# Feed-forward layers with their hidden features on the partitions, and a state-space unit whose scores follow its third chunk

## The chip, the cores and the metric

The kernel runs on one core of one Trainium2 chip. The metric is the time of one execution on the device, in microseconds (us). Before the change its median over three runs is 1958.67 us (1956.84 to 1959.5).

## What is computed

Two sequences (b = 0, 1) of 1024 tokens with 256 features pass through two layers. A layer normalises its input, computes a sequence mixer and a feed-forward network on the normalised input, and adds mixer × silu(network) to the residual. Layer 0 has linear attention (4 key heads, 16 query heads of 128) and a mixture of 8 experts (176 hidden features each, the two best per token) plus a shared expert of 352 hidden features. Layer 1 has a state-space model of 32 heads of 64 (a decayed running state) and a quantised feed-forward network with 704 hidden features.

```python
# layer 0's network
combine = zeros.at[token, topk_idx].add(topk_w)
act = silu(gu[..., :F]) * gu[..., F:]                       # F = 176, eight experts
y = einsum('tef,te,ehf->th', act, combine, down_weights)
y = y + (silu(sgu[:, :Fs]) * sgu[:, Fs:]) @ shared_down.T   # Fs = 352
# layer 1's network, with W = (wq - 128) * scale
_qlinear(silu(_qlinear(x, wq_gate, s_gate)) * _qlinear(x, wq_up, s_up), wq_down, s_down)
# layer 1's mixer, per head and step
states = states * dec + xt[..., None] * bt[:, :, None, :]
yt = einsum('bhpn,bhn->bhp', states, ct) + xt * D
```

## The kernel before

Each sequence goes through seven phases, and all engines meet at the end of each (`end_phase`): normalisation; layer 0's network; attention; its output projection, which also normalises for layer 1; layer 1's network; the state-space (SSM) phase; its output projection. The order of work on each engine is written out by hand and held together by semaphores. A full-precision product of the normalised input is made of three passes over halves of the operands (`three_passes`: hi·hi, hi·lo, lo·hi), so every weight has a hi part (made by ScalarE, ACT) and a lo part (made by GpSimd, POOL, with `split_lo`, or by VectorE, DVE).

**The two networks.** The hidden features are worked on in groups of 352 (`FG`): five groups in layer 0 (four pairs of experts and the shared expert), two in layer 1. For each group the loop runs over eight chunks of 128 tokens, with tokens on the partitions (`ffn_group`, L540 in TensorE's block). Per chunk TensorE (PE) does `gate_up` (2 × 6 matmuls with 352 columns, L491), `hid_turn` (three transposes of the hidden values, L519) and `down` (nine matmuls with 256 columns, L532). ACT does the silu (L854) and copies the transposed values (L860). DVE multiplies by the up part and by the expert's weight of the token, a scalar on each partition (L1208, L1212), makes the lo part (L1219), and adds the chunk's result to `gate` in SBUF (L1241). The gate/up weights of a group (704 KB) share the buffer `w_raw` with all other projections. In layer 1 DVE first dequantises them with the scales (L1250, L1465). The silu of the sum is taken in the next phase (L887).

**The SSM phase.** It runs over 16 pairs of heads, and each pair over two units u of four chunks. PE's order within a unit is `ssm_unit` (L794): per chunk j a projection `project_xz`, `ssm_update` (L778) and `ssm_outputs` (L787, L792); behind chunk 0 the next unit's `project_b`, behind chunk 1 its `project_c`; in chunk 2, between the projection and the update, its scores `unit_scores` (L768, 16 small matmuls); in chunk 3 the transposes `b_turn` (L751). The scores need ACT's copy `c_copy` (L1114), and ACT takes its steps in order too: in the first unit of a pair it also makes the hi part of the next pair's weights (`ssm_prep`, L838), for which `w_raw` must have landed. SP issues that load behind `pdec` (L372), and `pdec` waits for the state of the previous pair's last chunk (L1522, a memset on DVE). DVE's order in a unit is per chunk `ssm_next_state` (L1527), `add_skip` (L1539), then in chunks 0 and 1 a scan (L1499), in chunk 2 `c_decayed` (L1507) and `decayed_scores` of head 0 (L1515), in chunk 3 that of head 1. `ssm_outputs` of a chunk waits until `add_skip` has read the chunk before it out of the one PSUM bank, and `add_skip` waits for POOL's `xd` (L463), which stands in POOL's queue behind the lo part of the next weights (L473).

## Time and profile before

| | |
|---|---|
| median of three runs | 1958.67 us |
| the profiled execution, and its span | 1956.97 us, 1955.2 us |
| PE, weight loads, DVE, ACT, POOL busy | 91%, 81%, 60%, 43%, 31% of the span |
| granted TensorE clock, mean | 0.97 |
| chain that ended last | PE 63%, DVE 9%, issue 8%, DMA 7%, ACT 6%, POOL 4%, SP's queue 2% |
| DMA | 110.83 MB, 57 GB/s on average |

The busy share of PE alone says little, since the ends of matmuls are modelled and overlap; what counts is how far apart the starts of its instructions are and where it stands idle. The page cuts the span into 40 slices, and the same pattern of slices comes twice, once for each sequence.

### The profile page before, as it was taken

To read this page: it belongs to the slowest core of one execution; us is meant where nothing else is said; L and a number is where in the kernel's file an instruction comes from. 1 tells how busy PE (TensorE), PEld (TensorE's weight loads), DVE (VectorE), ACT (ScalarE), POOL (GpSimd) and SP (SyncE) were. 2 spreads that over 40 slices of the span, in tenths; PEclk is the share of its full clock that TensorE was granted. 3 is DMA by queue.
4 is the path that set the end of the run, shared out by engine and by line. 5 is a ranking of instruction groups with operands and counts; after the bars stand their busy time and mean duration, and the time that the engine had idled before them with its cause. 6 is when DMAs were issued, how large, how long until landed. Compare 5 with 4: busy or idle time off the path is not lost.

```text
span 1955.2 us, 33861 instructions
## 1 busy us (share of the span) xinstructions
PE 1783.1 (91%) x11888; PEld 1591.4 (81%) x11888; DVE 1178.2 (60%) x2476; ACT 843.7 (43%) x2294; POOL 611.6 (31%) x768
## 2 busy tenths in 40 slices
PE   5998999899899999998969979998988999999989
PEld 4997777788888888887849967777888888888878
DVE  5555888554456566666455558885554556666664
ACT  4234445323344444445533344453233444444465
POOL 1012444001255555551010124440002555555510
PEclk9999999999999999998969999999999999999989
DMA  2120000002322222220021200000023222222200
GB/s 81 47 105 17 17 17 24 11 1 74 89 90 90 90 90 90 90 92 10 12 80 40 105 17 18 17 24 11 1 74 90 90 90 90 90 91 94 90 6 17
DMA packets 49783, 110.83 MB, mean 57 GB/s; under 512 B 5712, under 2 KB 14544, under 8 KB 49104
## 3 DMA queue, kind: packets, MB, share of 16 engines
q1 hardware_dynamic: 49616, 108.66, 16.8%
q8 instruction: 98, 1.61, 0.3%
q14 instruction: 69, 0.57, 0.1%
HBM read 106.02 MB, written 2.62 MB: 56 GB/s over the span
## 4 chain that ended last, share of the span: by engine, by line
PE 63%; DVE 9%; issue 8%; DMA 7%; ACT 6%; POOL 4%; SPq 2%; DVEq 0%; POOLq 0%; ACTq 0%
PE ps L491 23%; PE ps L563 11%; DMA w_raw<-in_w_in 6%; PE ps L532 5%; PE ps L768 4%; PE ps L787 4%; PE ps L555 3%; PE ps L778 2%; POOL rb L417 2%; PE ps L663 2%; PE ps L644 2%; PE ps L519 2%; PE ps L664 2%; PE ps L792 2%; SPq L372 2%
## 5 line engine op out<-in xcount | busy, mean ns | idle before, releaser
L468 POOL TENSOR_TENSOR y<-yg,sz 128x128 f32<-128x128 f32 x256 | 209.8, 820 | 262.2 <-DVE yg L1539 262.2
L563 PE MATMUL ps<-w_out,yT 128*128 128x256 f32 x1024 | 226.1, 379 | 0.0
L1527 DVE SCALAR_TENSOR_TENSOR ssm_state<-ssm_state,pdec,ps 64x64 f32<-64x64 f32 x448 | 125.2, 279 | 165.7 <-PE ps L778 159.1
L563 PEld LDWEIGHTS ps<-w_out,yT 128*128 128x128 f32 x1024 | 192.5, 190 | 24.9
L417 POOL TENSOR_TENSOR rb<-ra,rb 128x512 f32<-128x512 f32 x80 | 118.6, 1482 | 221.9 <-DVE rb L1367 221.8
L787 PE MATMUL ps<-xz_x,mt 128*128 128x128 f32 x1024 | 167.5, 282 | 2.6 <-DVE mt L1515 1.4
L1499 DVE TENSOR_TENSOR_SCAN lmat<-dec,ident 128x512 f32<-128x512 f32 x128 | 155.9, 1218 | 0.4 <-issue 0.4
L491 PE MATMUL ps<-w_in_hi,xnT_hi 128*128 128x256 f32 x512 | 155.5, 304 | 0.0
L1539 DVE TENSOR_TENSOR yg<-ps,xd 128x128 f32<-128x128 f32 x256 | 74.6, 291 | 128.7 <-issue 88.8
L854 ACT ACTIVATE silu_g<-ps 128x352 f32<-128x352 f32 x112 | 51.7, 465 | 228.6 <-PE ps L491 228.5
L491 PE MATMUL ps<-gu_hi,xnT_hi 128*128 128x352 f32 x448 | 148.9, 332 | 0.0
L491 PE MATMUL ps<-gu_lo,xnT_hi 128*128 128x352 f32 x448 | 148.5, 331 | 0.0
L787 PEld LDWEIGHTS ps<-xz_x,mt 128*128 128x128 f32 x1024 | 140.5, 192 | 8.6 <-DVE mt L1515 6.7
L491 PE MATMUL ps<-gu_hi,xnT_lo 128*128 128x352 f32 x448 | 147.2, 329 | 0.0
L491 PE MATMUL ps<-w_in_lo,xnT_hi 128*128 128x256 f32 x512 | 144.2, 282 | 0.0
L491 PE MATMUL ps<-w_in_hi,xnT_lo 128*128 128x256 f32 x512 | 143.6, 280 | 0.0
L463 POOL TENSOR_TENSOR xd<-xz_x,d_row 128x128 f32<-128x128 f32 x256 | 122.5, 479 | 34.7 <-ACT xz_x L1126 34.7
L1131 ACT ACTIVATE xw<-ps,lmat 128x64 f32<-128x64 f32 x512 | 133.1, 319 | 0.0
L1126 ACT ACTIVATE xz_x<-ps 128x128 f32<-128x128 f32 x256 | 71.6, 280 | 141.1 <-PE ps L491 129.6
L1208 DVE SCALAR_TENSOR_TENSOR hid<-ps,combine_g,silu_g 128x176 f32<-128x176 f32 x160 | 56.3, 394 | 113.0 <-ACT silu_g L854 98.6
L473 POOL TENSOR_TENSOR w_in_lo<-w_raw,w_in_hi 128x256 fp32r<-128x256 f32 x120 | 87.3, 727 | 92.7 <-ACT w_in_hi L838 92.7
L1000 ACT ACTIVATE ra<-rb 128x512 f32<-128x512 f32 x80 | 50.4, 630 | 148.6 <-POOL rb L417 147.5
(170 smaller groups left out, 4809.1 us busy)
## 6 DMA issues: line engine op xcount, KB each, us to landing
dec<-dec_dram SPq DMA_DIRECT2D x64, 512.0 KB, 5.1
w_raw<-in_w_in SPq DMA_DIRECT2D x32, 512.0 KB, 4.3
pdec<-dec_dram SPq DMA_DIRECT2D x128, 128.0 KB, 2.9
w_raw<-in_gu SPq DMA_DIRECT2D x14, 704.0 KB, 4.2
w_raw<-in_w_qkv SPq DMA_DIRECT2D x8, 768.0 KB, 4.9
dn_raw<-in_dn SPq DMA_DIRECT2D x14, 384.0 KB, 4.8
w_out<-in_w_o SPq DMA_DIRECT2D x2, 2048.0 KB, 11.9
w_out<-in_w_out SPq DMA_DIRECT2D x2, 2048.0 KB, 8.5
```

What stands on the lines that cost most here:

```text
L417: nc.gpsimd.tensor_tensor(rb[:, k], ra[:, k], rb[:, k], ALU.add).then_inc(a_rot.sem, 1)
L463: nc.gpsimd.tensor_tensor(xd[:, s].rearrange("p (h c) -> p h c", c=64), xz_x[:, s, :].rearrange("p (h c) -> p h c", c=64)[:, 0:4:3, :], d_ ...
L468: nc.gpsimd.tensor_tensor(y[:, c, bass.ds((2 * i + w) * P, P)], yg[:, s], sz[:, s], ALU.mult).then_inc(s_out.sem, 1)
L473: ins = nc.gpsimd.tensor_tensor(w_in[1 - w][1][:, k, half], raw[:, k, half], w_in[1 - w][0][:, k, half], ALU.subtract)
L491: mm = nc.tensor.matmul(out, left(l, k), right(r, k), start=(j == 0), stop=(j == len(steps) - 1))
L532: mm = nc.tensor.matmul(ps[:, 6 + c % 2, 0:DM], hidT[l][:, c % 2, t * P:(t + 1) * P], dn[slot][r][:, t, :], start=(j == 0), stop=(j == len ...
L563: mm = nc.tensor.matmul(ps[:, 4 + s, 0:DM], yT[:, s, t, :], w_out[:, t, :], start=(t == 0), stop=(t == NT - 1))
L768: mm = nc.tensor.matmul(ps[:, 4 + h, j * P:(j + 1) * P], bT[q, toks], cT[q, toks], start=True, stop=True)
L787: nc.tensor.matmul(out, mt1[:, u % 2, h, c % 4 * P:(c % 4 + 1) * P], xz_x[:, c % 2, h * P:(h + 1) * P], start=(h == 0), stop=False)
L1131: ins = nc.scalar.activation(xw[:, s, 64 * h:64 * h + 64], ps[:, 2 + s, 64 * h:64 * h + 64], ACT.Copy, scale=lmat[:, h, (c + 1) * P - 1:(c ...
L1499: nc.vector.tensor_tensor_scan(lmat[:, h, toks], dec[:, h, toks], ident4[:, 0:HALF], 0.0, ALU.mult, ALU.add).then_inc(s_scan.sem, 1)
L1527: ins = nc.vector.scalar_tensor_tensor(ssm_state[q, nxt, q], ssm_state[q, cur, q], pdec[q, (c + 1) * P - 1:(c + 1) * P], ps[q, 7, q], ALU. ...
```

## The change

- **Networks.** The hidden features are now on the partitions: tiles of 128 features (14 in layer 0, of which three are the shared expert with 32 rows of padding in the third, and eleven hold the 8 × 176 expert features without a gap; 6 in layer 1, the last with 64 features whose gate and up rows share one product). Per tile and half of the tokens (a unit u) PE does 12 matmuls with 512 columns and 12 with 256; the result of all tiles is summed up in four PSUM banks. No transposes and no adding in SBUF are left.
- A token's weight for an expert is no longer a scalar on a partition. The table is transposed by PE once per sequence (8 matmuls), written to DRAM, and each expert tile loads its rows of it, broadcast over the partitions (`comb`, 512 KB per tile). POOL multiplies the silu by it.
- The weights of a tile (384 KB) have buffers of their own (`fw_raw`, two deep). ACT and POOL (layer 1: ACT and DVE) split them in two pieces, 512 and 256 columns wide, one in each unit. In layer 1 the zero point goes off while splitting, the scales are applied by the silu, by the split of the hidden values and in the last sum.
- In layer 0 the silu of the sum is taken at the end of the phase out of PSUM; in layer 1 DVE applies the last scale out of PSUM at the end of the phase.
- **SSM phase.** On PE `unit_scores` moves behind the update and the outputs of chunk 2. On DVE `decayed_scores` of head 0 moves from the end of chunk 2 to the start of chunk 3.
- Two constants (`s_gu`, `s_dn`) are loaded at the start. Logits of the router and of the decays use PSUM banks 2 and 3.

```diff
@@ TensorE: networks
-                for j in range(2):
-                    mm = three_passes(ps[:, 2 * (c % 2) + j, 0:FG],
-                                      lambda l, k: xnT[l][:, k, c * P:(c + 1) * P],
-                                      lambda r, k: weights[r][:, k, j * FG:(j + 1) * FG])
+                pe.wait_ge(f_hid.sem, f_hid.done(u - 2))
+                for j in range(1 if together else 2):
+                    mm = three_passes(ps[:, 2 * hf + j, :],
+                                      lambda l, kk: fw[k % 2][l][:, (2 * kk + j) * P:(2 * kk + j + 1) * P],
+                                      lambda r, kk: xnT[r][:, kk, hf * HALF:(hf + 1) * HALF])
...
+            def down(b, k, hf, first, last, rows=P):
+                pe.wait_ge(f_hi.sem, f_hi.done(u))
+                pe.wait_ge(f_lo.sem, f_lo.done(u))
+                for j in range(4):
+                    c = 4 * hf + j
+                    for x, (l, r) in enumerate(SPLITS):
+                        mm = nc.tensor.matmul(ps[:, 4 + c // 2, (c % 2) * DM:(c % 2 + 1) * DM], hidT[l][0:rows, hf, j * P:(j + 1) * P],
+                                              fw[k % 2][r][0:rows, KT * 2 * P:FW], start=(first and x == 0 and c % 2 == 0),
+                                              stop=(last and x == 2), skip_group_check=True)
...
+                gate_up(b, 0, 1)
+                for u in range(2 * NF0):
+                    if u == 2:
+                        pe.wait_ge(own_dve, 2 * b + 2)
+                        pe.wait_ge(f_hid.sem, f_hid.done(2 * b * NF + 2))
+                        for c in range(NC):
+                            mm = nc.tensor.matmul(ps[0:NE, c // 4, c % 4 * P:(c % 4 + 1) * P], combine[:, c, :], ident4[:, 0:P],
+                                                  start=True, stop=True)
+                        mm.then_inc(rt_combT.sem, 1)
+                        down(b, 1, 0, False, False)
+                        pe.wait_ge(rt_combcopy.sem, rt_combcopy.done(b))
+                        gate_up(b, 2, 0)
+                        continue
+                    if u + 2 < 2 * NF0:
+                        gate_up(b, (u + 2) // 2, u % 2)
+                    down(b, u // 2, u % 2, u < 2, u >= 2 * NF0 - 2)
@@ TensorE: SSM unit
-                        if ahead and j == 2:
-                            unit_scores(u + 1, nhf)
                         ssm_update(u, m, c)
                         ssm_outputs(u, m, c)
...
+                        if ahead and j == 2:
+                            unit_scores(u + 1, nhf)
@@ VectorE: SSM unit
+                        if ahead and j == 3:
+                            decayed_scores(u + 1, 0)
                         ssm_next_state(m, c)
                         add_skip(m, c)
...
                         if j == 2:
                             c_decayed(u + 1)
-                            decayed_scores(u + 1, 0)
@@ ScalarE: layer 0's network
+                for u in range(2 * NF0):
+                    k, hf = u // 2, u % 2
+                    if u > 0:
+                        silu(b, k, hf)
+                    if u == 2:
+                        act.wait_ge(rt_combT.sem, rt_combT.done(b))
+                        nc.scalar.activation(comb_T[:].rearrange("p (h t) -> p h t", h=2), ps[0:NE, 0:2, :], ACT.Copy).then_inc(rt_combcopy.sem, 1)
+                    hidden_hi(b, k, hf)
+                    if hf == 0 and k + 1 < NF0:
+                        weights_hi0(b, k + 1, 0)
+                    if hf == 1 and k + 1 < NF0:
+                        weights_hi0(b, k + 1, 1)
@@ GpSimd: layer 0's network
+                for k in range(NF0):
+                    e = k - SHARED_TILES
...
+                    for hf in range(2):
+                        u = 2 * (b * NF + k) + hf
+                        if e >= 0:
+                            pool.wait_ge(f_silu.sem, f_silu.done(u))
+                            nc.gpsimd.tensor_tensor(silu_g[:, hf, :], silu_g[:, hf, :], comb[:, e % 2, hf * HALF:(hf + 1) * HALF], ALU.mult).then_inc(f_comb.sem, 1)
+                        if k + 1 < NF0:
+                            weights_lo(k + 1, hf)
@@ VectorE: networks
+                nc.vector.tensor_tensor(hid[0:rows, hf, :], up, silu_g[0:rows, hf, :], ALU.mult).then_inc(f_hid.sem, 1)
...
+                    ins = nc.vector.tensor_tensor(hidT[1][0:rows, hf, :], hid[0:rows, hf, :], hidT[0][0:rows, hf, :], ALU.subtract)
@@ SP: layer 0's network
+                for k in range(NF0):
+                    ffn_weights(b, k, a["fw0"][F0[k]])
...
+                    if k >= SHARED_TILES:
+                        e = k - SHARED_TILES
+                        sp.wait_ge(f_comb.sem, f_comb.done(2 * (b * EXPERT_TILES + e - 2) + 1))
+                        for x, (row, p0, p1) in enumerate(expert_rows(F0[k])):
+                            sp.dma_start(comb[p0:p1, e % 2, :], comb_dram[row:row + 1, :].broadcast_to([p1 - p0, T])).then_inc(comb_in[e % 2], 16)
@@ ScalarE: layer 1's network
+                for u in range(2 * NF1):
+                    silu(b, NF0 + k, hf, s_gu[0:rows, k, 0:1], rows)
+                    hidden_hi(b, NF0 + k, hf, s_gu[0:rows, k, 1:2], rows)
+                    if k + 1 < NF1:
+                        weights_hi1(b, k + 1, hf)
+                    if k == NF1 - 1 and hf == 0:
+                        first_pair()
```

## Rows read from the trace of the kernel before

**Rows 1.** Busy time by stage: PE, PEld, DVE, ACT, POOL, granted clock, DMA share.

```profile
22.30:171.30 149.00, 142.70 (x981) 136.28 (x981) 80.04 (x182) 47.85 (x95) 16.81 (x8) 0.99 0.15 55
...
440.20:512.70 72.50, 63.89 (x396) 61.04 (x396) 34.59 (x61) 22.29 (x40) 7.70 (x5) 0.89 0.31 92
512.70:897.60 384.90, 359.85 (x2784) 326.87 (x2784) 232.07 (x532) 177.91 (x624) 202.65 (x316) 1.00 0.26 84
```

**Rows 2.** Timeline of PE, layer 0's network: start us, us, what, [idle before].

```profile
41.14 0.32 PE L491 MATMUL ps<-gu_hi,xnT_hi 128*128 128x352 f32 x1
...
43.07 0.49 PE L519 MATMUL ps<-ident,hid 128*128 128x128 f32 x3
...
44.47 0.32 PE L491 MATMUL ps<-gu_hi,xnT_hi 128*128 128x352 f32 x1
```

**Rows 3.** Timeline where PE or ACT stood idle in both networks and behind.

```profile
35.91 0.90 PE L519 MATMUL ps<-ident,hid 128*128 128x128 f32 x3 [4.51 <-DVE hid L1208]
...
181.87 1.28 ACT L887 ACT_TABLE_LOAD   x1
...
465.47 0.55 PE L519 MATMUL ps<-ident,hid 128*128 128x128 f32 x3 [2.77 <-DVE hid L1212]
...
496.09 1.06 ACT L838 ACTIVATE w_in_hi<-w_raw 128x1024 fp32r<-128x1024 f32 x1 [7.80 <-issue]
...
498.11 0.90 PE L519 MATMUL ps<-ident,hid 128*128 128x128 f32 x3 [4.03 <-DVE hid L1212]
```

**Rows 4.** Groups of instructions: xcount | busy us, mean ns | idle before.

```profile
L473 POOL TENSOR_TENSOR w_in_lo<-w_raw,w_in_hi 128x256 fp32r<-128x256 f32 x120 | 87.3, 727 | 92.7 <-ACT w_in_hi L838 92.7
L1515 DVE TENSOR_TENSOR mt<-ps,lmat 128x512 f32<-128x512 f32 x128 | 86.8, 680 | 0.7 <-PE ps L768 0.7
...
L768 PE MATMUL ps<-cT,bT 64*128 64x128 f32 x1024 | 74.5, 285 | 43.8 <-ACT cT L1114 43.8
...
L389 POOL TENSOR_TENSOR w_qkv_lo<-w_raw,w_qkv_hi 128x512 fp32r<-128x512 f32 x24 | 30.4, 1285 | 58.3 <-ACT w_qkv_hi L838 58.3
...
L838 ACT ACTIVATE w_qkv_hi<-w_raw 128x512 fp32r<-128x512 f32 x24 | 14.0, 625 | 0.0
```

**Rows 5.** Timeline of PE in one pair of SSM heads.

```profile
632.26 1.16 PE L768 MATMUL ps<-cT,bT 64*128 64x128 f32 x16
633.35 0.49 PE L778 MATMUL ps<-xw,b_tok 128*128 128x128 f32 x2
...
644.22 1.16 PE L768 MATMUL ps<-cT,bT 64*128 64x128 f32 x16 [1.08 <-ACT cT L1114]
...
645.63 0.61 PE L787 MATMUL ps<-xz_x,mt 128*128 128x128 f32 x4
...
646.30 0.60 PE L751 MATMUL ps<-ident,bT 128*128 128x128 f32 x4
```

**Rows 6.** Timeline of SP, DVE, ACT and POOL in the same pair.

```profile
637.37 0.58 SPq L303 DMA_DIRECT2D w_raw<-in_w_in  x1
...
633.98 0.57 DVE L1527 SCALAR_TENSOR_TENSOR ssm_state<-ssm_state,pdec,ps 64x64 f32<-64x64 f32 x2 [2.31 <-PE ps L778]
...
636.04 0.17 DVE L1522 MEMSET ssm_state<- 128x128 f32 x1
...
643.76 0.29 DVE L1539 TENSOR_TENSOR yg<-ps,xd 128x128 f32<-128x128 f32 x1 [2.69 <-issue]
...
641.39 1.06 ACT L838 ACTIVATE w_in_hi<-w_raw 128x1024 fp32r<-128x1024 f32 x1 [3.44 <-DMA w_raw<-in_w_in]
...
643.22 0.45 POOL L463 TENSOR_TENSOR xd<-xz_x,d_row 128x128 f32<-128x128 f32 x1
```

**Rows 7.** Timeline of POOL and of DVE, one stretch in which both work.

```profile
72.95 3.25 POOL L389 TENSOR_TENSOR gu_lo<-w_raw,gu_hi 128x1408 fp32r<-128x1408 f32 x1 [24.18 <-ACT gu_hi L838]
...
73.63 3.38 DVE L1223 TENSOR_TENSOR dn_lo<-dn_raw,dn_hi 128x768 fp32r<-128x768 f32 x1 [0.87 <-ACT dn_hi L879]
```

**Rows 8.** Part 6 of the page, DMA issues: count, KB each, us to landing.

```profile
dec<-dec_dram SPq DMA_DIRECT2D x64, 512.0 KB, 5.1
```

More of the change, by code:

```diff
@@ L39 @@
 FE = 176
-FG = 2 * FE
-G0, G1 = NE // 2 + 1, 2
-GRP = G0 + G1
-DT = 3
+SHARED = 2 * FE
+NF0 = 14
+EXPERT_TILES = NE * FE // P
+F0 = tuple(range(EXPERT_TILES, NF0)) + tuple(range(EXPERT_TILES))
+SHARED_TILES = NF0 - EXPERT_TILES
+HID = 704
+NF1 = 6
+NF = NF0 + NF1
+FW = KT * 2 * P + DM
 HP = 16
@@ L54, with expert_rows @@
 PHASES = 7
-CONSTS = 7
-RAWS = G0 + KVH + G1 + HP
+CONSTS = 9
+RAWS = KVH + HP
 PARTS = 3
-def split_ffn0(b, g):
-    return b * (RAWS + (PARTS - 1) * KVH) + g
 def split_qkv(b, i, part):
-    return split_ffn0(b, G0) + PARTS * i + part
-def split_ffn1(b, k):
-    return split_qkv(b, KVH, 0) + k
+    return b * (PARTS * KVH + HP) + PARTS * i + part
 def split_ssm(b, h):
-    return split_ffn1(b, G1) + h
+    return b * (PARTS * KVH + HP) + PARTS * KVH + h
+def expert_rows(tile):
+    f, rows = tile * P, []
+    while f < tile * P + P:
+        end = min((f // FE + 1) * FE, tile * P + P)
+        rows.append((f // FE, f - tile * P, end - tile * P))
+        f = end
+    return rows
+COMB_LOADS = [sum(len(expert_rows(t)) for t in range(k, EXPERT_TILES, 2)) for k in range(2)]
 class Event:
@@ L536, in ffn_group, with gate_up @@
-            def ffn_group(b, g, slot, weights, split, last=False):
-                for c in range(NC):
-                    if c + 2 < NC or not last:
-                        g2, c2 = following(g, c, 2)
-                        gate_up(b, g2, c2, weights[c + 2 >= NC], split + (c + 2 >= NC))
-                    if c + 1 < NC or not last:
-                        hid_turn(b, *following(g, c, 1))
-                    down(b, g, c, slot)
+            def gate_up(b, k, hf, together=False):
+                n = b * NF + k
+                u = 2 * n + hf
+                if hf == 0:
+                    pe.wait_ge(f_wgh.sem, f_wgh.done(n))
+                    pe.wait_ge(f_wgl.sem, f_wgl.done(n))
+                pe.wait_ge(f_hid.sem, f_hid.done(u - 2))
[3 more added lines that the diff above has]
+                                      lambda r, kk: xnT[r][:, kk, hf * HALF:(hf + 1) * HALF])
+                mm.then_inc(f_gu.sem, 1)
@@ L1607, in launch_arrays, with tile_rows @@
     g["router"] = np.concatenate([rows_to_k(f["L0_ffn_gate_weight"]).reshape(P, -1), np.zeros((P, DM - KT * NE), np.float32)], 1)
-    def groups(gate_up, down):
-        gus = np.stack([rows_to_k(x).reshape(P, -1) for x in gate_up])
-        dns = np.stack([rows_to_k(np.concatenate([x, np.zeros((DM, DT * P - FG), x.dtype)], 1)).reshape(P, -1) for x in down])
-        return gus, dns
+    def tile_rows(gate, up, down):
+        return np.concatenate([rows_to_k(np.concatenate([gate, up])).reshape(P, -1), np.concatenate([down.T, np.full((P - down.shape[1], DM), PAD, down.dtype)])], 1)
@@ L1623, in launch_arrays @@
+    g["s_gu"] = scales.transpose(1, 0, 2)
     g["s_dn"] = f["L1_ffn_s_down"].reshape(1, DM)
```

445 lines of the change are left out of this document (184 added, 261 removed).

## The prediction

> **What bounds the kernel now.** I read three views in this order. First the stages [rows 1]. In the SSM phase PE is busy for 360 of 385 us at full clock. In layer 1's network it is busy for 64 of 72.5, at a granted clock of 0.89. So PE is the bound, with idle stretches, and what is worth something is work taken from PE, or idle time of it.
>
> Second the timeline of PE. In layer 0's network a chunk of 128 tokens takes 44.47 - 41.14 = 3.33 us from start to start [rows 2]. Its 12 gate/up matmuls take 43.07 - 41.14 = 1.93 us, that is 0.161 each or 0.457 ns a column; by the column a matmul of 512 columns takes 0.234 and one of 256 takes 0.117 (estimates from that row). Nine down matmuls are then 1.05, so the three transposes and their change of operand cost 0.35 us of PE in each chunk. The idle stretches are 4.5 us behind the router, while DVE ranks the experts, and 2.8 and 4.0 us in layer 1's network [rows 3]. In the second of these ACT sat in its queue at the SSM phase's first weights for 7.8 us, and silus stood behind them.
>
> Third the SSM phase. PE waits 43.8 us before the scores for ACT's cT [rows 4], once per pair of heads (384.9 / 16 = 24.06 us a pair). The pair at 632 us shows the loop that sets this [rows 5, 6]: DVE clears the state of the last chunk (636.04), only then SP may issue pdec and behind it the weights (637.37), these land before 641.39 (ACT waited 3.44), ACT splits them, then come its copies of the chunk and of b and c, and PE starts its scores at 644.22 after 1.08 us of idling. POOL's xd at 643.22 and DVE's yg at 643.76 hang on the same landing. Over the two sequences 14 pairs each do so, a mean of 43.8 / 28 = 1.56 us.
>
> **Layer 0's network, work of PE.** Before: 40 chunks of 3.33 = 133.2 us. After: 14 tiles of 24 × 0.234 + 24 × 0.117 = 8.42, together 117.9. That is -15.3 per sequence. The loads of weights into PE fall from 24 per chunk to 48 per tile and hide as before.
>
> **Its start.** The 4.5 us idle stretch goes. What is late next: ACT now loads the table of silu, of exp and of silu again (1.28 us each, as the row at 181.87 in [rows 3]), and DVE's first product stands ahead of the ranking, so that the second gate/up product waits some 1.2 us for DVE to have read the logits; the third waits for the weights that ACT splits only behind exp: 1.5 us. Then comes the turned table of expert weights: 8 small products of two passes each (16 × 0.11 = 1.8 us by the 0.35 / 3 of a transpose), and in this unit ACT copies the table (about 1.0) before it may make the hi part of the hidden values, so that PE's next down product waits: copy 1.0, hi 0.63, lo 0.68 and handovers = 2.5. Sum -4.5 + 1.2 + 1.5 + 1.8 + 2.5 = +2.5 (between 0 and +6). The four small waits between groups (not shown; between 0 and 2 in all) count as -1.5.
>
> **The expert tiles: a ring through four engines.** Here I expect the new bound. POOL's product with `comb` must be between silu and DVE's product, ACT takes silu, hi part and the weights' hi part in that order, and POOL's lo part of the weights stands ahead of its next product. With durations from [rows 4] (ACT 512 columns 0.63, POOL 512 columns 1.28, 256 columns 0.73, DVE 0.68, hand-over about 0.07, ACT overlapping its next start by 0.1), counted from the end of POOL's product: DVE's product until 0.82, ACT's hi until 1.52, DVE's lo part until 2.27; ACT's weights until 2.05 (512 wide) or 1.8. Can POOL work beside DVE's lo part, which reads two SBUF operands? No [rows 7]: DVE's step at 73.63 took 3.38 us instead of some 1 us, ending 0.8 behind POOL's at 72.95 + 3.25; so the later of the two waits for the earlier one's end. So POOL begins at 2.2: 2.2 + 1.28 + 1.28 = 4.76 in the first unit, 2.2 + 0.73 + 1.28 = 4.21 in the second, 8.97 a tile against PE's 8.42. Eleven tiles × 0.55 = +6.0 per sequence. Lower bound 0 (POOL beside DVE: 4.6 + 3.8 = 8.4, PE is the bound again); upper bound with POOL's products held once more for a DVE step of 0.68 in each unit +1.4 a tile, +21. I take 6.0, since DVE has no second step of that kind in the unit.
>
> The Trainium skill (SBUF — State Buffer, section "Who interferes with whom") says that a VectorE instruction with two SBUF inputs and a GpSimd one that reads SBUF exclude each other for a whole instruction, while one with a single SBUF input doesn't. The trace agrees with the first half; by the second half DVE's product out of PSUM costs the ring nothing more. Without that rule the ring would be 8.4 and the forecast 12 us lower.
>
> **Its end.** The sum's silu out of PSUM stands behind the last product (two of 0.53, where one short addition stood): +1.1, an estimate. In return the attention phase loses a silu of 1.9 us and a table load there and back (the row at 181.87 in [rows 3]); it lay partly beside other work: -1.3 (0 to -4.5).
>
> **The broadcast loads** of `comb` are hidden: 512 KB took 5.1 us to land for `dec` [rows 8], they are issued when tile k-2 frees the buffer, three units (13 us) ahead of use, and the weights of the next tile (384 KB) go with them. Without that cover each tile would cost the landing, 5 us or more.
>
> **Layer 0's network in sum:** -15.3 + 2.5 - 1.5 + 6.0 + 1.1 - 1.3 = -8.5 per sequence.
>
> **Layer 1's network.** PE: before 16 × 3.33 = 53.3; after 132 × 0.234 + 144 × 0.117 = 47.7: -5.6. Both idle stretches go, -6.8: the weights come in pieces, and the SSM weights are awaited only beside the last tile, 8 units after their chain has begun. Part of the clock lost with them comes back: 0.11 of 72.5 us is missing, 5 us of it at half clock behind the start; I count -2.0. Against it: the second tile's weights are split behind the first tile's hidden values, 1.5; the last sum takes four DVE steps of 0.68 where a short addition stood, two of them behind PE's end: +1.5. POOL is out of this ring, whose ACT part is about 2.4 us against a unit of 4.21. Sum -11.4 (-7 to -14).
>
> **SSM phase.** After the change PE does the update and outputs of chunk 2 while it would have waited. The update can go at once (ACT copies its inputs ahead of b and c). The outputs need yg of chunk 1, read at 643.76 + 0.29 = 644.05: nearly the time at which cT came. So of the stall only the update is hidden: outputs from 644.12, 0.67 (645.63 to 646.30), scores 1.09 (644.22 to 645.31 is their share before), b_turn at 645.9 instead of 646.30: 0.40 earlier. The second gain is in the other unit of the pair, which has no stall. There the memset of the state came 3.78 us behind the start of the scores (632.26 to 636.04), because update, state step, yg and the masks followed them. Now update and outputs go first: state step at 0.63 behind the slot's start (633.35 to 633.98 before), yg at 1.2, c at 1.45, mask at 2.2 (as soon as the scores end at 2.15), memset at 2.87: 0.91 earlier, and with it SP's pdec and the weights. The loop shrinks by 1.31 us per pair; the stall had 1.56 on average, so it doesn't run dry. 14 × 1.31 = -18.3 per sequence. DVE's order is the same as before (head 0's mask stands right before chunk 3's state step in both). Nobody waits longer for the masks: the next unit's outputs come 0.7 and more behind them.
>
> **Normalisation and start:** two more constants ahead of x (each at most the 0.58 that SP took at 637.37 in [rows 6]), shorter splits beside the normalisation: 0 (-3 to +1).
>
> **Sum:** (-8.5 - 11.4 - 18.3) × 2 = -76.4. The profiled execution took 1956.97 (span 1955.2), so 1880.6; the median of three was 1.7 higher. I give 1881.
>
> **Rivals.** (a) PE is the bound everywhere: POOL isn't held by DVE (-6.0 per sequence) and the remaining SSM stall of 0.25 to 0.7 goes too (-5). For it: POOL's wait needs an exact overlap, and DMA landings vary. 1881 - 22 = 1859. (b) The scores' move gives only scraps: the loop is closed by something that doesn't move, such as POOL's queue, and 0.4 per pair is left: 28 × 0.9 = +25, 1906. For it speaks yg at 643.76, tied to the landing; against it that the landing itself follows the memset. (c) The expert ring is longer, 10 us a tile, by slow POOL steps: +23, 1904. (d) Slower than before: the gate on TensorE's clock. In layer 1's network, with 2.8 and 4.0 us of idling, the clock is 0.89; in the SSM phase with 1.1 us it is 1.00 [rows 1, 3, 5]. If the ring's idle parts (0.55 a tile) drop the clock, a tile takes 16.8 us: 11 × 2 × 7.9 = +173, 2054. It makes the kernel slower from 10 of the 22 tiles on. Against it: the stall per tile is smaller than those at clock 1.00.
>
> The Trainium skill (TensorE: Matmul & The Clock Gate, section "A second HAM failure mode: psum-queue depth-cycling") speaks for (d): short idling between groups of matmuls let the clock swing. The SSM rows here, with such gaps at 1.00, don't show it.
>
> **Chances.** Forecast 0.55 (1868 to 1893), (a) 0.20, (b) 0.13, (c) 0.08, (d) 0.04. The range 1843 to 1908 holds the forecast, most of (a), (b) and (c). What this kernel's measurement can tell from no change is about 0.2%. Faster 0.95, same 0.01, slower 0.04.
>
> **What would show it.** Layer 0's network (149.0) at about 140, expert tiles 9.0 apart, POOL's comb products starting as its weight step ends; layer 1's at 61 without idling at its SSM weights; the pair of heads at 22.7 with 0.2 to 0.7 of stall ahead of the outputs or scores; the memset 2.9 behind the update. Wrong if a tile takes 8.4 or over 9.5, if the stall before the scores stays above 1 us, or if landings of `comb` are waited for.

## The result, and the profile after

| | before | after |
|---|---|---|
| median | 1957.76 us (four runs) | 1885.9 us (1884.98 to 1886.98) |
| profiled execution, its span | 1956.97, 1955.2 | 1884.98, 1883.2 |
| ratio of times, 95% interval | | 0.9636 (0.9619 to 0.9653) |
| PE, DVE, ACT, POOL busy | 91%, 60%, 43%, 31% | 93%, 58%, 45%, 36% |

The forecast was 1881 (1843 to 1908). By phases, each cut where the last of ACT, DVE and POOL drains, first and second sequence:

| us | before | after | difference | forecast |
|---|---|---|---|---|
| normalisation | 22.3, 19.1 | 22.6, 15.8 | +0.3, -3.3 | 0 |
| layer 0's network | 148.9, 150.8 | 141.3, 140.7 | -7.6, -10.1 | -7.2 |
| attention | 190.9, 192.5 | 192.1, 191.4 | +1.2, -1.1 | -1.3 |
| layer 1's network | 72.6, 72.3 | 60.8, 61.1 | -11.8, -11.2 | -11.4 |
| SSM | 384.8, 384.1 | 370.5, 371.2 | -14.3, -12.9 | -18.3 |
| the two output projections | 157.2, 157.1 | 156.0, 156.9 | -1.2, -0.2 | 0 |

The stages of the changed kernel, first sequence (us of the stretch, busy time with counts, granted clock, DMA share, GB/s), against [rows 1]:

```profile
22.62:163.94 141.32, 130.83 (x708) 109.64 (x708) 45.44 (x68) 54.51 (x95) 61.00 (x52) 0.97 0.32 105
433.73:494.57 60.84, 55.08 (x288) 46.64 (x288) 30.52 (x45) 26.43 (x39) 3.38 (x2) 0.93 0.37 113
494.57:865.10 370.53, 361.23 (x2784) 326.96 (x2784) 230.78 (x532) 177.82 (x624) 203.04 (x316) 0.99 0.27 87
```

PE is busy for 361 of 370.5 us in the SSM phase where it was busy for 360 of 385: no work went, idle time did. In layer 1's network 55 of 60.8 us are left of 64 of 72.5.

**The expert tiles don't close at 8.97 us.** PE's down products of one half start at 86.82, 95.33 and 103.83: 8.50 us a tile. Timeline of POOL, DVE and ACT in one tile (start, duration, what, [idle before]):

```profile
95.37 0.94 POOL L396 TENSOR_TENSOR fw_lo<-fw_raw,fw_hi 128x256 fp32r<-128x256 f32 x1 [1.77 <-ACT fw_hi L873]
96.27 1.30 POOL L411 TENSOR_TENSOR silu_g<-silu_g,comb 128x512 f32<-128x512 f32 x1
99.56 1.29 POOL L396 TENSOR_TENSOR fw_lo<-fw_raw,fw_hi 128x512 fp32r<-128x512 f32 x1 [1.99 <-ACT fw_hi L870]
100.80 1.29 POOL L411 TENSOR_TENSOR silu_g<-silu_g,comb 128x512 f32<-128x512 f32 x1
...
95.02 0.69 DVE L1203 TENSOR_TENSOR hidT_lo<-hid,hidT_hi 128x512 fp32r<-128x512 f32 x1 [0.70 <-ACT hidT_hi L862]
97.60 0.69 DVE L1196 TENSOR_TENSOR hid<-ps,silu_g 128x512 f32<-128x512 f32 x1 [1.89 <-POOL silu_g L411]
99.00 0.69 DVE L1203 TENSOR_TENSOR hidT_lo<-hid,hidT_hi 128x512 fp32r<-128x512 f32 x1 [0.70 <-ACT hidT_hi L862]
...
98.33 0.63 ACT L862 ACTIVATE hidT_hi<-hid 128x512 fp32r<-128x512 f32 x1 [2.20 <-DVE hid L1196]
99.77 0.60 ACT L856 ACTIVATE silu_g<-ps 128x512 f32<-128x512 f32 x1 [0.29 <-PE ps L497]
```

From the end of POOL's product (96.27 + 1.30 = 97.57) DVE's product starts after 0.03, ACT's hi part after 0.76, DVE's lo part ends after 2.12 (99.00 + 0.69), POOL's 512-wide step starts at 1.99 and its next product ends at 4.52 (102.09). The other half takes 3.97, the sum is 8.50. The silu isn't on this chain: ACT waits 0.29 us for PE in front of it, and it still ends (100.37) 0.43 before POOL's product starts. But PE's own work is as long as the chain. A tile of the shared expert, which has no product on POOL, takes 8.48 us (PE's down products start at 61.33 and at 69.81). PE and the ring are level.

**The end of layer 0's network** has a stall that I had not foreseen. ACT waits 3.58 us for the first attention head's weights, two silus stand behind it, and PE then idles 3.53 us. SP had issued that load behind the tables and w_o, 3 MB in all, and it took 11.9 us to land. The clock falls in the idle time (0.89 on average between 152.0 and 155.7), and the last two groups of down products take 2.5 us each instead of 1.41. Timeline of ACT, then of PE:

```profile
149.88 1.67 ACT L840 ACTIVATE w_qkv_hi<-w_raw 128x512 fp32r<-128x512 f32 x3 [3.58 <-DMA w_raw<-in_w_qkv]
...
155.70 0.55 PE L533 MATMUL ps<-fw_hi,hidT_hi 128*128 128x256 f32 x1 [3.53 <-DVE hidT_lo L1203]
```

The stretch of the first group behind it (us of the stretch, busy times, granted clock, DMA):

```profile
155.70:158.20 2.50, 2.50 (x12) 2.50 (x12) 0.79 (x2) 0.63 (x1) 2.50 (x4) 0.50 0.00 0
```

**Start of the SSM phase.** The first projections run at half clock. Their starts are 0.43 apart, at full clock 0.23. In the kernel before they ran at a clock of 1.00. Timeline of PE:

```profile
495.21 0.63 PE L497 MATMUL ps<-xnT_lo,w_in_hi 128*128 128x512 f32 x1
495.64 0.63 PE L497 MATMUL ps<-xnT_hi,w_in_lo 128*128 128x512 f32 x1
```

**A pair of heads.** The mean period is 23.0 us (24.1 before). The stall before the scores [rows 5] is gone, and a smaller one stands before the outputs of chunk 2: the update starts at 647.11 and the outputs only at 647.77, 0.66 later, where it is 0.22 at the other chunks, so 0.44 is lost; the distances of starts in excess of the usual make 7.2 us at this place in the first sequence and 8.1 in the second. What it waits for can be followed backwards: yg at 647.34, POOL's xd at 646.78, behind POOL's lo part of the weights at 646.08, behind ACT's hi part, behind the landing of weights that SP issued only after the memset. Timeline of the engines in this order of steps, headed by the update of the unit before:

```profile
636.36 0.38 PE L780 MATMUL ps<-xw,b_tok 128*128 128x128 f32 x2
...
639.22 0.17 DVE L1477 MEMSET ssm_state<- 128x128 f32 x1
...
640.54 0.58 SPq L306 DMA_DIRECT2D w_raw<-in_w_in  x1
...
644.95 1.06 ACT L840 ACTIVATE w_in_hi<-w_raw 128x1024 fp32r<-128x1024 f32 x1 [2.87 <-DMA w_raw<-in_w_in]
...
646.08 0.74 POOL L479 TENSOR_TENSOR w_in_lo<-w_raw,w_in_hi 128x256 fp32r<-128x256 f32 x1 [2.21 <-ACT w_in_hi L840]
646.78 0.47 POOL L469 TENSOR_TENSOR xd<-xz_x,d_row 128x128 f32<-128x128 f32 x1
...
647.34 0.29 DVE L1494 TENSOR_TENSOR yg<-ps,xd 128x128 f32<-128x128 f32 x1 [2.13 <-issue]
...
647.11 0.38 PE L780 MATMUL ps<-xw,b_tok 128*128 128x128 f32 x2
647.77 0.68 PE L789 MATMUL ps<-xz_x,mt 128*128 128x128 f32 x4 [0.28 <-DVE yg L1494]
...
649.70 0.66 PE L753 MATMUL ps<-ident,bT 128*128 128x128 f32 x4
```

### The profile page after: what moved, and what is told of

Same layout as the page of the kernel before. It is cut to its first block, busy times and chain, and to the rows that moved or that the text cites. A ratio compares the mean times of both kernels' runs of the same rounds, so it can differ in the third digit from the quotient of the medians.

```text
span 1883.2 us, 31983 instructions
## 1 busy us (share of the span) xinstructions
PE 1742.3 (93%) x11128; PEld 1506.7 (80%) x11128; DVE 1091.5 (58%) x2215; ACT 854.1 (45%) x2288; POOL 679.6 (36%) x846
## 4 chain that ended last, share of the span: by engine, by line
PE 54%; issue 15%; DVE 14%; POOL 10%; ACT 5%; DMA 2%; SPq 1%; POOLq 0%; DVEq 0%; ACTq 0%
PE ps L497 20%; PE ps L554 12%; PE ps L789 4%; PE ps L546 3%; POOL silu_g L411 3%; PE ps L533 2%; PE ps L770 2%; POOL y L474 2%; PE ps L794 2%; POOL rb L429 2%; DVE yg L1494 2%; POOL fw_lo L396 2%; PE ps L664 2%; PE ps L665 2%; PE ps L645 2%
## 5 line engine op out<-in xcount | busy, mean ns | idle before, releaser
L1196 DVE TENSOR_TENSOR hid<-ps,silu_g 128x512 f32<-128x512 f32 (+1 forms) x80 | 55.2, 690 | 171.7 <-POOL silu_g L411 105.6
L396 POOL TENSOR_TENSOR fw_lo<-fw_raw,fw_hi 128x512 fp32r<-128x512 f32 (+1 forms) x56 | 62.7, 1120 | 249.3 <-ACT fw_hi L870 198.7
L497 PE MATMUL ps<-xnT_hi,fw_hi 128*128 128x512 f32 x312 | 125.8, 403 | 8.1 <-DVE fw_lo L1214 3.8
L497 PE MATMUL ps<-xnT_lo,fw_hi 128*128 128x512 f32 x312 | 124.6, 399 | 0.0
L497 PE MATMUL ps<-xnT_hi,fw_lo 128*128 128x512 f32 x312 | 124.0, 397 | 0.0
L497 PE MATMUL ps<-xnT_hi,w_in_hi 128*128 128x512 f32 x256 | 113.5, 443 | 4.5 <-DVEq L295 3.8
```

Source lines behind the costliest of these rows:

```text
L396: nc.gpsimd.tensor_tensor(fw[k % 2][1][:, cols], fw_raw[:, k % 2, cols], fw[k % 2][0][:, cols], ALU.subtract).then_inc(lo.sem, 1)
L497: mm = nc.tensor.matmul(out, left(l, k), right(r, k), start=(j == 0), stop=(j == len(steps) - 1))
```

## The experiments

The kernels were timed in three groups, each on one chip beside the kernel before, whose medians there were 1952.4, 1951.3 and 1949.2 us. The changed kernel, run again in the last group, has 0.9641 (0.9623 to 0.966), where it had 0.9636. A difference of ratios below is taken from 0.9638, times 1951 us. Each ratio's interval is some 3 us wide to either side, so a difference of two is uncertain by some 4. The lengths of phases and pairs come from one profiled execution of each kernel: the changed kernel's first one took 1885.0 us, that in the last group 1877.9.

### The scores' move, undone and alone

**Undone.** `unit_scores` stands again ahead of `ssm_update` and `ssm_outputs` of chunk 2, in both units of a pair:

```diff
+                        if ahead and j == 2:
+                            unit_scores(u + 1, nhf)
                         ssm_update(u, m, c)
                         ssm_outputs(u, m, c)
...
-                        if ahead and j == 2:
-                            unit_scores(u + 1, nhf)
```

> The changed kernel with the SSM scores back in their old place (ahead of the update and outputs of chunk 2); the networks stay as changed. By the forecast's own terms the move is worth 0.40 + 0.91 = 1.31 us a pair of heads, 36.6 us in all: 1885.9 + 36.6 = 1922.5 us. Rival 1: the move is worth less, 16.0 us a sequence (the phase became 13.6 shorter, and 2.4 us of that phase went to projections at half clock, which the networks' change brings and which stays here): 1918 us. Rival 2: the move is worth only the 13.6 us by which the phase shrank: 1913 us.

Measured: 0.9799 (0.9783 to 0.9815), that is +31.4 us. Rival 1 (32) fits; the 36.6 doesn't, and rival 2 (27) lies at the edge. Read the other way this is the kernel before with the networks' change alone: -39.2 us, where the forecast's two network terms make 39.8.

**Alone.** The same move made in the kernel before.

> The kernel before with the SSM move alone. Forecast: 1957.8 - 36.6 = 1921.2. Rival 1 (16.0 a sequence): 1925.8. Rival 2 (13.6 a sequence): 1930.6. Together with e1: if the parts are independent, the ratios of e1 and e4 multiply to that of the whole change, 0.9636. Here the SSM phase's first projections should run at full clock, as before.

Measured: 0.9837 (0.9822 to 0.9852), -31.8 us; rival 1 fits again, and the 36.6 lies outside the interval. The two ratios multiply to 0.9639: the parts add up. The SSM phase of the first sequence with the move alone (columns as in the first fence; before it is 384.9 at a clock of 1.00 [rows 1], after it 370.5 at 0.99, above):

```profile
515.20:881.00 365.80, 358.38 (x2784) 325.38 (x2784) 231.06 (x532) 178.03 (x624) 202.92 (x316) 1.00 0.27 89
```

The same phase in the changed kernel with the old order:

```profile
490.60:879.90 389.30, 363.67 (x2784) 330.00 (x2784) 231.66 (x532) 177.42 (x624) 202.44 (x316) 0.98 0.25 83
```

Both sequences together: 769.0 before and 733.9 with the move alone; 775.3 in the changed kernel with the old order and 741.8 with the new. So the move took 35.1 us from this phase in the one kernel and 33.5 in the other, where the forecast said 36.6. The networks' change made the phase longer, by 6.3 with the old order and by 7.9 with the new; some of this is the difference between executions, since the changed kernel in the last group has 736.9.

The mean clock of 1.00 in [rows 1] hides a part of this gain. From memset to memset a pair takes 23.87 us on average before and 22.78 with the move alone, 1.10 less, if the pairs in which the granted clock falls are left out. There are two of these before, 26.64 and 26.38 us long, and one with the move alone, of 25.63. In front of the two before, PE had waited 2.80 and 2.55 us for cT, the longest such waits there. For the first of them the timeline of PE, and the stretch behind it (columns as above):

```profile
669.39 1.16 PE L768 MATMUL ps<-cT,bT 64*128 64x128 f32 x16 [2.80 <-ACT cT L1114]
```

```profile
669.00:679.00 10.00, 9.59 (x67) 9.00 (x68) 6.81 (x15) 3.50 (x14) 6.58 (x10) 0.83 0.18 58
```

**One unit at a time.** The condition `and hf == 0` or `and hf == 1` on the moved call, the other unit's call back in front:

> The changed kernel with the scores moved only in the first unit of each pair of heads (chunks 0 to 3, the one in which PE waited for ACT's cT); in the second unit they are back in front. Forecast: this drops the 0.91 us a pair that came from the state being cleared earlier, 25.5 us: 1911.4. Rival: the gain sits in the first unit, where the update and the outputs fill the stall, and the second unit's order matters little: 1886 to 1890.

> The changed kernel with the scores moved only in the second unit of each pair (chunks 4 to 7, after which the state is cleared). Forecast: this drops the 0.40 us a pair, 11.2 us: 1897.1. Rival (the gain sits in the first unit): 1908 to 1913. If the two terms add up, what e2 and e3 lose sums to what e1 loses.

Measured: without the second unit's move 0.9776 (0.976 to 0.9791), +26.9 us, 0.96 per pair where the forecast had 0.91. Without the first unit's move 0.9629 (0.9615 to 0.9644), -1.8 us with an uncertainty of about 4: nothing, where the forecast had +11.2, and the rival, which had the gain in the first unit, is out. Together the two lose 25.1 us, where the old order in both units loses 31.4. The 6.3 between them is hardly more than the uncertainty, and long pairs are in it: with the old order three pairs have a fall of the clock, without the second unit's move one. The other pairs are 23.90 and 23.91 us long, so undoing the first unit's move as well costs nothing more. The first unit of a pair in the kernel without the first unit's move, ACT's split and PE's `b_turn`:

```profile
645.80 1.06 ACT L842 ACTIVATE w_in_hi<-w_raw 128x1024 fp32r<-128x1024 f32 x1 [3.25 <-DMA w_raw<-in_w_in]
...
650.71 0.60 PE L753 MATMUL ps<-ident,bT 128*128 128x128 f32 x4
```

From the start of ACT's split to `b_turn` it takes 650.71 - 645.80 = 4.91 us, in the changed kernel 649.70 - 644.95 = 4.75: the moved scores gain 0.16, not 0.40, as yg keeps the outputs waiting. At the memset nothing of it is left (17.04 us behind the split's start against 17.07).

### The ring, made longer

POOL makes each product with `comb` a second time, into a tile that nobody uses:

```diff
+                            nc.gpsimd.tensor_tensor(rt_gt[:].rearrange("p a e -> p (a e)"), silu_g[:, hf, :], comb[...], ALU.mult)
                             nc.gpsimd.tensor_tensor(silu_g[:, hf, :], silu_g[:, hf, :], comb[...], ALU.mult).then_inc(f_comb.sem, 1)
```

> The changed kernel with POOL's product with comb made twice in every unit of the expert tiles (the extra one goes to a scratch tile and is not used): 1.25 us more in the ring, per unit. In the changed kernel a tile takes 8.50 us, and POOL's products start right behind its split steps. If the ring has no slack left beside PE, a tile takes 8.50 + 2.5 = 11.0: 1885.9 + 55 = 1941. If PE alone sets 8.50 and the ring has the 0.25 us a unit that ACT waits for PE in front of each silu, 10.5: 1930. By the forecast's ring of 8.97, 11.5: 1952.

Measured: 0.9879 (0.9856 to 0.9902), +47 us; layer 0's network takes 165.7 and 165.9 us, +24.8 per sequence, 2.3 a tile on average. POOL's product that counts (L412; the extra one, L411, isn't shown) at the start of one tile and of the next:

```profile
107.00 1.28 POOL L412 TENSOR_TENSOR silu_g<-silu_g,comb 128x512 f32<-128x512 f32 x1
...
117.94 1.28 POOL L412 TENSOR_TENSOR silu_g<-silu_g,comb 128x512 f32<-128x512 f32 x1
```

The middle of the phase as one stretch:

```profile
70.00:170.00 100.00, 82.39 (x440) 70.05 (x439) 25.60 (x37) 27.92 (x55) 64.77 (x55) 0.97 0.35 115
```

The tile is 117.94 - 107.00 = 10.94 us long: the ring had hardly any slack (less than 0.1) and took nearly the whole 2.5. What it also shows: POOL's step of 256 columns takes 0.94 us here and in the changed kernel, where it overlaps DVE's lo part (95.37 against 95.02 + 0.69), and 0.73 for the same width alone [rows 4]. So DVE does hold POOL up, but by 0.2, less than the 0.34 that was left of DVE's step. By the rule of the Trainium skill cited in the prediction (SBUF — State Buffer, section "Who interferes with whom") it would have been all of it; the measurement decides.

The clock: PE is busy for only 82 of the 100 us here, and its granted clock is 0.97 on average. That mean hides falls. Between 65 and 170 us PE idles 2.24 to 2.26 us ahead of seven products of this ring; behind two of them (at 78.60 and 133.52) the clock goes to half for a while, behind the other five it doesn't. Timeline of PE for one of each, and the stretches behind them:

```profile
78.60 0.47 PE L498 MATMUL ps<-xnT_hi,fw_hi 128*128 128x512 f32 x1 [2.26 <-issue]
...
100.68 0.47 PE L498 MATMUL ps<-xnT_hi,fw_hi 128*128 128x512 f32 x1 [2.24 <-issue]
```

```profile
78.60:83.60 5.00, 5.00 (x17) 4.04 (x18) 1.38 (x2) 1.43 (x3) 3.23 (x3) 0.66 0.27 90
100.70:105.70 5.00, 5.00 (x28) 4.32 (x29) 1.38 (x2) 1.42 (x3) 3.23 (x3) 1.00 0.20 66
```

The tile with the fall takes 12.4 us and the next one 9.7, together only 0.2 more than twice 10.94: PE takes the lost time out of the idle time that it has here.

### Three orders

**The first head's weights earlier.** SP issues them ahead of tile 12's weights, not behind the tables and the 2 MB of w_o:

```diff
                 for k in range(NF0):
+                    if k == NF0 - 2:
+                        weights(split_qkv(b, 0, 0), a["w_qkv"][0], KT * QKV)
                     ffn_weights(b, k, a["fw0"][F0[k]])
...
-                for i in range(0, KVH):
+                for i in range(1, KVH):
```

> The changed kernel with one transfer moved: SP issues the first attention head's weights (768 KB) ahead of the weights of layer 0's tile 12, instead of behind the tables and the 2 MB of w_o. In the changed kernel they land at 149.88, ACT waits 3.58 us for them with two silus behind, and PE idles 3.69 us (3.63 in the second sequence) before the down products of tile 13. If that wait is the cause, both stalls go: 1885.9 - 7.3 = 1878.6. Rival: what is late next (POOL's products with comb behind its split steps, or w_raw competing with the loads of comb) keeps most of it: 1884 to 1886.

Measured: 0.9572 (0.9555 to 0.9589), -12.9 us; the phase takes 138.3 and 136.1 us, 7.6 less in both together. The 3.7 us stall is gone (stalls here are distances of starts in excess of the usual), and the one before the last down products grew from 1.6 to 2.7, since its silu and its product no longer had time to spare. The rest of the ratio's gain stands in phases that the edit doesn't touch, and its own five runs spread from 1863.4 to 1875.0, so I go by the phases. Both sequences idle alike before the last down products, but the clock falls only in the first. The first down product of each, and then the stretches behind it:

```profile
155.52 0.55 PE L535 MATMUL ps<-fw_hi,hidT_hi 128*128 128x256 f32 x1 [2.52 <-DVE hidT_lo L1205]
...
1088.50 0.35 PE L535 MATMUL ps<-fw_hi,hidT_hi 128*128 128x256 f32 x1 [2.54 <-DVE hidT_lo L1205]
```

```profile
155.50:158.00 2.50, 2.48 (x11) 2.50 (x12) 0.00 (x0) 0.00 (x0) 1.01 (x1) 0.50 0.36 44
1088.40:1091.00 2.60, 1.67 (x12) 1.49 (x12) 0.00 (x0) 0.80 (x2) 1.09 (x1) 1.00 0.25 45
```

**The next pair's weights earlier.** In the SSM phase SP issues them behind the first half's `pdec`:

```diff
-                    weights(split_ssm(b, h), a["w_in"][h], KT * XZBC)
+                    if h == 0:
+                        weights(split_ssm(b, h), a["w_in"][h], KT * XZBC)
...
                         for k in range(2):
                             sp.dma_start(pdec[64 * k:64 * k + 64, toks], ...).then_inc(pdec_in[hf], 16)
+                        if hf == 0 and h + 1 < HP:
+                            weights(split_ssm(b, h + 1), a["w_in"][h + 1], KT * XZBC)
```

> The changed kernel with SP's order in the SSM phase changed: the next head pair's weights are issued behind the first half's pdec, not behind the second half's, which waits for the state to be cleared. ACT waits 42.6 us per sequence for them now (3.0 a pair). Theory of the loop (memset, pdec, weights, split, scores, memset): it is cut, the waits before the outputs (7.2 us a sequence), before the scores (5.4) and the longer pairs of 23.6 to 24.1 go, the period falls from 23.0 to about 22.0: 1885.9 - 28 = 1858. Rival 1: PE's own work is the bound at 22.6 and only the odd pairs gain: 1875 to 1880. Rival 2: the transfers then collide with dec and pdec, which become what is awaited: 1886 or more.

Measured: 0.951 (0.9497 to 0.9522), -25 us; pairs are 22.00 us apart, nearly all of them. One stretch of the phase:

```profile
515.00:840.00 325.00, 324.62 (x2579) 298.37 (x2577) 217.88 (x491) 164.66 (x578) 187.71 (x294) 1.00 0.28 94
```

PE is busy for 324.6 of 325 us. The loop is shown: memset, pdec, weights and split set the pace, and with the weights issued ahead of the memset PE does.

**With the old order of the scores**, and the same early issue of the weights.

> The changed kernel with the SSM scores back in their old place, but with the next pair's weights issued behind the first half's pdec. Theory: the scores' move was worth 28 to 32 us only because it shortened the loop memset, pdec, weights, split, scores, memset; with that loop cut by the earlier issue, PE sets the pair at 22.0 us in either order: the ratio to the kernel before is that of the changed kernel with the early issue alone, 0.951, within 0.002. Rival: the move is also worth something by itself, as update and outputs fill the wait for ACT's cT: 0.957 or more (0.4 us a pair).

Measured: 0.9567 (0.9553 to 0.9581). My theory missed: with the loop cut the move is still worth 0.0057, 11 us. But the rival's mechanism isn't it either: PE has no wait for cT left. PE's own pitch differs, 22.27 against 22.00 us a pair. Timeline of PE in one unit with the new order:

```profile
570.01 0.28 PE L500 MATMUL ps<-w_in_hi,xnT_lo 128*128 128x256 f32 x1
570.13 0.38 PE L783 MATMUL ps<-xw,b_tok 128*128 128x128 f32 x2
...
571.11 1.16 PE L773 MATMUL ps<-cT,bT 64*128 64x128 f32 x16
572.21 0.66 PE L756 MATMUL ps<-ident,bT 128*128 128x128 f32 x4
572.62 0.36 PE L500 MATMUL ps<-w_in_hi,xnT_hi 128*128 128x256 f32 x1
```

The same in the old order:

```profile
571.39 0.28 PE L500 MATMUL ps<-w_in_hi,xnT_lo 128*128 128x256 f32 x1
571.65 1.16 PE L773 MATMUL ps<-cT,bT 64*128 64x128 f32 x16
572.74 0.49 PE L783 MATMUL ps<-xw,b_tok 128*128 128x128 f32 x2
...
573.74 0.60 PE L756 MATMUL ps<-ident,bT 128*128 128x128 f32 x4
574.10 0.36 PE L500 MATMUL ps<-w_in_hi,xnT_hi 128*128 128x256 f32 x1
```

The same instructions lie between the last projection pass in front and the first one behind: 572.62 - 570.01 = 2.61 us against 574.10 - 571.39 = 2.71, and all units between 515 and 840 us that have both ends in this stretch are alike to 0.01. In each unit the scores are the only products of 64 rows (64*128), the others have 128. Time goes where the shape changes. Going into the scores takes 0.14 more than a pass in the old order (571.39 to 571.65, where a pass is followed after 0.12), and the update behind them 0.11 more than in the new (0.33 to the outputs' start against 0.22); with `b_turn` behind them instead it is 0.05 (0.41 against 0.36), and in front 0.09 (0.31 behind the last outputs against 0.22). The Trainium skill (TensorEngine Tiling (Array Packing), section "Key Properties") says that a change of the tiling mode drains TensorE. The trace agrees in so far as the distances of starts are longer at these places. But both orders have two such changes in a unit, and no run here separates the change of shape from other causes, nor why one order pays 0.1 more. By the pitch of the pairs it is 0.27 × 28 = 8 us; the 11 come from ratios of two groups, uncertain by some 4.

**The hi part before the table's copy.**

```diff
                     if u == 2:
+                        hidden_hi(b, k, hf)
                         act.wait_ge(rt_combT.sem, rt_combT.done(b))
                         nc.scalar.activation(comb_T[:]..., ACT.Copy).then_inc(rt_combcopy.sem, 1)
-                    hidden_hi(b, k, hf)
+                    else:
+                        hidden_hi(b, k, hf)
```

> The changed kernel with ACT's hi part of the hidden values of unit 2 ahead of its copy of the turned table (1.01 us). If the 2.60 us that PE idles there come from that order, the idle time falls to 1.6; the next gate/up product then waits for the copy, which is hidden behind the down product of 1.4. Rival: it stays at 2.6, since the hi part waits for DVE's product, which comes late anyway.

Timeline of PE at that place, L396 being POOL's lo part of the weights:

```profile
48.85 0.47 PE L497 MATMUL ps<-xnT_hi,fw_hi 128*128 128x512 f32 x1 [1.54 <-POOL fw_lo L396]
```

The 2.6 us stall in front of the down product is gone, not just 1.0 of it, and 1.7 stand in front of the next gate/up product, which waits not for the copy but for POOL's lo part: tile 2's weights stood behind the copy on ACT. The phase takes 139.4 and 138.9 us, 1.8 less in each sequence. There is one execution of this kernel, and its time of 1871.6 us is not used.

**All three, with tile 2's weights also ahead of the copy.**

> The changed kernel with three orders changed: the first attention head's weights issued ahead of tile 12, the next head pair's weights in the SSM phase issued behind the first half's pdec, and ACT's copy of the turned table put behind its hi parts of unit 2 and of tile 2's weights. From the runs with the first two alone -7 and -25 us, and for the third the whole stall of 2.6 in each sequence, -5: 1885.9 - 37 = 1849, ratio 0.945. If the third only moves the stall to the next gate/up product, as with the hi part alone (1.70 us there), 1852.

Measured: 0.946 (0.9447 to 0.9473), median 1843.9, that is -34.7 us against the changed kernel. Layer 0's network takes 134.2 and 133.8 us; at the table PE no longer idles.

### The clock behind layer 1's network

As the last kernel, and PE computes 5 unused products ahead of the last down products and 8 behind them:

```diff
                     down(b, NF0 + u // 2, u % 2, ...)
+                    if u >= 2 * NF1 - 2:
+                        for x in range(5 if u == 2 * NF1 - 2 else 8):
+                            nc.tensor.matmul(ps[:, 0, :], xnT[0][:, 0, 0:P], xnT[0][:, 0, 0:HALF], start=True, stop=True)
```

> As the kernel with three orders, and in layer 1's network PE computes 5 unused products of 512 columns ahead of the last down products and 8 behind them, in a bank that nobody reads, where it idled 1.3 and 2.1 us. In the changed kernel the SSM phase's first projections run at half clock (granted clock 0.53 in the 6 us from 494). If the idling in front of them lets the clock fall, it stays at full speed and each sequence gains up to 2.8 us: 5.6 us less than the kernel with three orders. Rival: the clock falls all the same, no difference; or the filler delays the end of the phase, slower by 1 to 3.

Measured: 0.9436 (0.9421 to 0.945), -4.7 us against the last kernel, median 1839.3. The projections run at full clock. Timeline of PE, the filler (L740), the first projection and what follows the twelfth:

```profile
483.67 2.11 PE L740 MATMUL ps<-xnT_hi 128*128 128x512 f32 x8
486.12 0.47 PE L502 MATMUL ps<-xnT_hi,w_in_hi 128*128 128x512 f32 x1 [0.34 <-PEq L295]
...
489.00 0.28 PE L502 MATMUL ps<-w_in_hi,xnT_hi 128*128 128x256 f32 x1
```

The twelve take 489.00 - 486.12 = 2.88 us, in the kernel without the filler 5.05 (from 486.13 to 491.18). So the idle time let the clock fall, and that cost 2.2 us per sequence. This is the fastest of the kernels: 2.1% under the changed one by the ratios (0.9436 / 0.9638 = 0.979).

## Why the prediction was right, and which steps were not

The total was forecast at 38.2 us per sequence and came to 36.0. The largest terms were right in kind and nearly in size, but that the total is so close is in part luck. Averaged over the sequences, the SSM phase gave 13.6 where 18.3 were forecast, and attention nothing where 1.3 were. Against this stand 8.9 for 7.2 in layer 0's network, where two misses nearly cancel, and 1.5 and 0.7 in the normalisation and the output projections, where nothing was forecast and which no run explains.

- **Layer 0, work of PE.** Forecast 14 × 8.42; measured 8.50 a tile (8.48 where no product on POOL stands in it), 119.0 instead of 117.9. Held, but for 1.1 (-14.2 for -15.3).
- **Layer 0, start.** Forecast +2.5 with stalls of 1.2, 1.5 and 2.5; measured 1.14, 0.58 + 0.76 and 2.60. Held, and the run with the hi part first shows that the last is what it was said to be.
- **The expert ring: the step that failed.** Forecast 8.97 a tile, measured 8.50, so +6.0 became about 0: rival (a) in this half. The forecast let POOL's step begin at 2.2 and then take its full length (by its own sum DVE's lo part ended at 2.27). Measured, hand-overs take 0.03 to 0.04 us instead of 0.07, so the lo part ends at 2.12. And POOL isn't held until then: its steps end at 3.28 and 2.71, as if they had begun at 2.00 and 1.98 and taken the usual 1.28 and 0.73. Its following step starts 0.04 before the one in front has ended. That is 0.24 in each unit, 0.47 a tile: some 0.08 by the hand-overs, 0.12 to 0.14 by the hold, 0.04 by the overlap. [rows 7] had the sign of it: DVE's step ended 0.8 behind POOL's, less than the 1 us that the prediction gave it alone. The run with the product twice shows the ring with a slack of less than 0.1, so PE and ring meet at 8.50.
- **Small waits between groups.** Forecast -1.5; the starts of chunks are 4.01 to 4.11 apart at four places instead of 3.34, so they were worth 2.9.
- **Layer 0, end: the other step that failed.** I asked what stands behind ACT's silus in the old layer 1 [rows 3] and didn't ask it of the new layer 0, where the same pattern had come in: the next phase's weights are awaited ahead of the last silus, and SP had 3 MB in front of them. It cost 3.7 us of idling and 2.2 of half clock in the last down products, against +1.1 forecast. With the terms as measured the phase would be 7.6 us shorter (-14.2 + 2.5 - 2.9 + 3.7 + 2.2 + 1.1); it is 8.9 on average, and the 1.3 between are not assigned.
- **Attention.** The gain of 1.3 didn't come (+1.2 and -1.1): its first projections run at half clock too (0.50 from 163.9 to 168.0, where the kernel before had 1.00), behind the idle end of layer 0.
- **Layer 1's network.** Forecast -11.4, measured -11.8 and -11.2. In the first sequence PE's busy time fell by 8.8, where work and clock were forecast at 7.6, and the rest of the phase by 2.9, where idle stretches and what stands against them made 3.8. No run tests these terms one by one.
- **SSM.** The memset held: 639.22 - 636.36 = 2.86 behind the update, forecast 2.87. The two terms made 1.31 a pair; measured in the kernel before it is 1.10 in pairs without a fall of the clock, which makes 30.7 us; 2.4 more of the -35.1 come from two long pairs at half clock becoming one, so that this sum lies so near the forecast's 36.6 is luck. The division was wrong: the second unit's term is 0.96 per pair, the first unit's is nil next to it, because the outputs wait for yg (0.44 at 647.77) and had been taken to start at once. The forecast also left out that PE's own work gets shorter by the new order, 0.27 a pair once the loop is cut. In the changed kernel the phase gained only 27 of the 35: the half clock of the first projections (2.2 per sequence, removed by the filler) is the part that is shown. The other 1.8 per sequence are within what profiles of the same kernel differ by (the changed kernel's second one has 369.7 and 367.2 where the first has 370.5 and 371.2). Single pairs of 23.3 to 24.1 us stand among those of 22.5 to 22.9 there. With the weights issued earlier nearly all of them are gone, so they hang on the loop; the clock doesn't fall in them, and what made them long stays open.
- **Rival (d)**, the clock in the ring: tiles of 16.8 us didn't come. In the changed kernel the ring leaves PE no idle time that the timeline shows, so its condition wasn't met. With the product twice it was, by 2.2 us in a tile; the clock fell behind two of seven such stretches and came back, and the mean was 0.97. So the fall does happen, but doesn't last. The prediction set the SSM phase's clock of 1.00 against it, which is a mean too, with two falls in it. And the clock fell where idle stretches stand at the end of a phase, which I had counted nowhere.

## What to carry to other kernels

When a phase gets shorter, ask of its end what was asked of the old one: which engine takes its step for the next phase, where in its queue that stands, and how many bytes are in front of the transfer that it waits for. Look at what order SP issues in before moving work on the compute engines: one load moved on SP was worth 25 us, nearly as much as the scores' move (31). And before costing a ring, see how near it is to the engine beside it: three sizes of 0.04 to 0.14 us in a unit decided here which one was the bound. Look behind a mean clock as well: 1.00 over 385 us and 0.97 over 100 both had falls to half in them.

## What the hardware did that I had not expected

- The same idle time need not have the same effect on the clock. Before the last down products PE idled 2.52 us in one sequence and 2.54 in the other; behind it the granted clock was 0.50 and 1.00. With the product twice it idled 2.26 and 2.24 us in front of two like products; behind them the clock was 0.66 and 1.00.
- The order of products costs PE time without any wait: 0.1 us per unit, with the products of 64 rows in another place.
- POOL and DVE: a POOL step that started 0.34 us before DVE's instruction with two SBUF inputs ended was 0.2 us longer (0.94 for 0.73), one that started 0.13 before its end took 1.29, no longer than without.
